# A four-part transformer block on one core: the second half of the tokens moved beside the first half's expert chunks

## The reference, cut to what matters

```python
x = x + tanh(g_xattn[0]) * wkv(w, u, k=layernorm(x), v=ctx)          # scan over the 256 tokens of a sequence
x = x + tanh(g_ffn[0])   * ffn(layernorm(x))                         # 256 -> 1024 -> 256, ternary weights, 8-bit activations
x = x + tanh(g_xattn[1]) * attention(layernorm(x), ctx)              # 32 heads of 8, rms-normed q and k, softmax over 256 keys
x = x + tanh(g_ffn[1])   * moe(layernorm(x))                         # 64 experts of width 64, top 8, one shared expert

def moe(x):
    logits = x @ gate_w.T
    W = softmax over the top 8 logits, zero elsewhere                # (tokens, 64)
    gate, up = x @ gu_w                                              # every expert on every token
    out = (silu(gate) * up * W) @ dp_w
    return out + sigmoid(x @ sh_gate1_w.T) * shared_expert(x)
```

## Time and profile before

| | us |
|---|---|
| runs before (3) | 525.39 median, 525.39 to 528.26 |
| the profiled execution | 525.49 |
| its span, from the first to the last record | 523.7 |
| busy PE / DVE / ACT / POOL | 405.8 / 340.7 / 293.1 / 23.7 |
| mean granted clock of PE | 0.94 |
| DMA | 38.01 MB, mean 73 GB/s |

### The profile page before, as it was taken

The page is one execution under the profiler, slowest core; times in us unless marked ns, Lnnn a source line. Parts: engine busy times, 40 slices in busy tenths (PEclk is TensorE's granted clock), DMA queues, the critical chain, the costliest instruction groups (busy, mean ns, idle before and its releaser), DMA issues.

```text
span 523.7 us, 7357 instructions
## 1 busy us (share of the span) xinstructions
PE 405.8 (77%) x2606; PEld 194.0 (37%) x2606; DVE 340.7 (65%) x723; ACT 293.1 (56%) x447; POOL 23.7 (5%) x21
## 2 busy tenths in 40 slices
PE   1104237448666798877799999999999999999994
PEld 1002123225443343433345444444444444444442
DVE  6899399884875554756497477566565565554553
ACT  2992894757787889887455254443333434423321
POOL 0002051002000111000000000000000000000000
PEclk9999856968999889998799999999999999999999
DMA  8400000000002000004520345633433433312211
GB/s 308 167 0 0 1 0 1 1 0 1 0 3 61 0 3 2 2 11 130 169 83 26 108 129 166 175 101 113 141 103 109 140 111 102 131 60 72 70 61 40
DMA packets 24576, 38.01 MB, mean 73 GB/s; under 512 B 4826, under 2 KB 11354, under 8 KB 24028
## 3 DMA queue, kind: packets, MB, share of 16 engines
q1 hardware_dynamic: 24540, 37.54, 22.7%
HBM read 36.21 MB, written 1.31 MB: 72 GB/s over the span
## 4 chain that ended last, share of the span: by engine, by line
PE 58%; ACT 16%; DVE 14%; issue 8%; DMA 2%; POOL 1%; SPq 1%; ACTq 0%; DVEq 0%
PE ps L1133 34%; PE ps L1406 15%; ACT regA L639 4%; ACT regA L467 1%; PE ps L1125 1%; PE ps L1190 1%; ACT regA L470 1%; PE ps L1155 1%; PE ps L1333 1%; DVE xn L762 1%; DMA regA<-in_dp_dram 1%; PE ps L1290 1%; DVE bn L748 1%; DMA x<-in_x_dram 1%; ACT regB L531 1%
## 5 line engine op out<-in xcount | busy, mean ns | idle before, releaser
L1133 PE MATMUL ps<-hH,regB 128*128 128x512 f16 x512 | 164.0, 382 | 0.0
L691 ACT ACTIVATE regA<-ps 128x512 f32<-128x512 f32 x65 | 38.8, 597 | 146.7 <-PE ps L1133 144.9
L1091 DVE TENSOR_TENSOR regA<-ps,regA 128x512 f32<-128x512 f32 x65 | 45.0, 692 | 100.2 <-ACT regA L691 100.2
L1133 PE MATMUL ps<-hL,regB 128*128 128x512 f16 x256 | 97.8, 382 | 0.0
L1406 PE MATMUL ps<-regA,regB 128*128 128x512 f16 x384 | 93.3, 379 | 1.3 <-DVE regA L1096 1.3
L1133 PEld LDWEIGHTS ps<-hH,regB 128*128 128x128 f16 x512 | 50.4, 98 | 61.7 <-issue 2.9
L639 ACT ACTIVATE regA<-ps 128x1024 f32<-128x1024 f32 x64 | 62.0, 1025 | 10.0 <-PE ps L1320 9.1
L1406 PEld LDWEIGHTS ps<-regA,regB 128*128 128x128 f16 x384 | 37.3, 98 | 47.3 <-DVE regA L1096 2.4
L1096 DVE TENSOR_TENSOR regA<-regA 128x512 f16<-128x512 f32 x65 | 44.3, 682 | 0.7 <-ACT regA L683 0.7
L1101 DVE TENSOR_TENSOR regA<-regA 128x512 f32<-128x512 f32 x65 | 44.5, 685 | 0.0
L683 ACT CAST regA<-regA 128x512 f16<-128x512 f32 x65 | 39.6, 610 | 1.5 <-DVE regA L1101 1.5
(11 more groups left out here) (169 smaller groups left out, 498.4 us busy)
## 6 DMA issues: line engine op xcount, KB each, us to landing
regA<-routing_dram SPq DMA_DIRECT2D x130, 128.0 KB, 3.1
regA<-in_gu_dram SPq DMA_DIRECT2D x32, 256.0 KB, 2.6
regA<-in_dp_dram SPq DMA_DIRECT2D x32, 128.0 KB, 2.7
regA<-in_ffn_dram SPq DMA_DIRECT2D x2, 1024.0 KB, 8.2
x<-in_x_dram SPq DMA_DIRECT2D x2, 512.0 KB, 3.9
ctxT<-in_ctxT_dram SPq DMA_DIRECT2D x1, 1024.0 KB, 8.2
regB<-in_ffn_dram SPq DMA_DIRECT2D x1, 1024.0 KB, 12.2
out_dram<-x SPq DMA_DIRECT2D x2, 512.0 KB, 3.3
```

The source lines that it names most:

```text
L691: nc.scalar.activation(sgm[:, c % 2, :], bank(GATE_BANK[c % 2]), ACT.Silu, scale=UNSCALE).then_inc(esilu_done, 1)
L1091: V.tensor_tensor(sgm[:, c % 2, :], bank(GATE_BANK[c % 2] + 1), sgm[:, c % 2, :], ALU.mult).then_inc(et_done, 1)
L1133: mm = T.matmul(out_ap, w(k), a(k), start=(n == 0), stop=(n == 3 * DK - 1))
```

## The change

It rewrites the order of the whole kernel. What is computed, and in what precision, stays the same but for two roots (below).

1. Halves. All stages up to the routing run for the first half of the tokens (tiles 0 to 3), with the second half's scan between its attention groups and the second half's wide products of tile 4. Then the chunks start: 32 pairs on half 0, the shared expert, 32 pairs on half 1. Beside chunks 0 to 27 lie the second half's FFN (tiles 5 to 7 and the rest of 4), its q and k/v projections, its 32 score units and 16 weighted values, heads, norms and routing. Three tables say what each engine does in places A, B and C of a chunk.
2. Weights. NW is 9. 8 pairs are kept from half 0 to half 1; the other 24 are fetched and split again (57 entries instead of 33).
3. Banks. In chunks 0 to 32 gate and up have banks 2 and 3 alone (every chunk), half 0's accumulators 0 and 1, the beside work 4 to 7. From chunk 33 on they alternate between 6, 7 and 2, 3; half 1's accumulators are 4 and 5. Gate and up now signal one by one.
4. Table loads. In chunks 11 to 22 and 26 silu is computed by tanh (same table as exp): ACT's tanh(z/2), DVE (1 + tanh) * gate, then times up: one more DVE operation.
5. POOL has no work. Row splits go to DVE (`split_low`); the ternary weights are clamped on DVE (`ternary_weights`, five operations of 2048 columns), with one ACT Relu; `drop_magic` goes. Second-half row turns are copied out by ACT. For scan chunks 2 and 3 DVE clamps (`clamps`) what ACT's Relus of the second pair did.
6. From norm 8 and row run 4 on, the inverse root starts from an integer guess on DVE (`bits_root`) and takes three Newton steps there, without ACT.

```diff
-        SHARED = NW
-        CHUNKS = [(p, 0) for p in range(NW)] + [(p, 1) for p in range(NW)] + [(SHARED, 2)]
-        CHUNKS += [(p, h) for p in range(NW + 1, PAIRS - NW) for h in range(2)]
-        CHUNKS += [(p, 0) for p in range(PAIRS - NW, PAIRS)] + [(p, 1) for p in range(PAIRS - NW, PAIRS)]
+        KEPT = NW - 1
+        LATER = [SHARED - KEPT + j for j in range(KEPT)] + list(range(SHARED - KEPT))
+        CHUNKS = [(p, 0) for p in range(SHARED)] + [(SHARED, 2)] + [(p, 1) for p in LATER]
...
+        ENTRY_PAIR = list(range(PAIRS)) + LATER[KEPT:]
+        SPLIT_AT = {e: e - EARLY if e < PAIRS else e + 4 for e in range(EARLY, ENTRIES)}
+        for e in range(NS + EARLY, ENTRIES):
+            LOAD_IN[SPLIT_AT[e - NS] + 3] = e
...
+        BESIDE_SCALAR = {
...
+            (10, "B"): [("table_exp_tanh",), ("probabilities", 32, 4), ("probabilities", 33, 6)],
+            (11, "A"): [("probabilities", 34, 4), ("probabilities", 35, 6)],
...
+        BESIDE_VECTOR = {
...
+            (5, "C"): [("row_sums", 10), ("row_sums", 11), ("rows", 5), ("norm", 9)],
...
+            (7, "C"): [("split_low", 11), ("row_sums", 12), ("row_sums", 13), ("weights_low", 10), ("rows", 6)],
...
+            (10, "C"): [("row_sums", 15), ("split_low", 13), ("rows", 7)],
...
+            (22, "C"): [("heads_sum", 31, 5), ("low_halves", 10, 6), ("weights_low", 28), ("heads_out", 6, 4),
+                ("heads_out", 7, 6), ("stats", 11), ("norm", 11)],
...
+        BESIDE_PRODUCTS = {
...
+            (5, "B"): [("project", 10, 7), ("project", 11, 6)],
+            (5, "C"): [("project", 12, 7), ("project", 13, 6)],
...
+            (13, "A"): [("scores", 39, 6), ("weighted_values", 18, 5)],
...
+        BY_TANH = tuple(range(11, 23)) + (26,)
+
+        def gate_bank(c):
+            return 6 if c > SHARED and (c - SHARED) % 2 else 2
+
+        ACC = (0, 4)
...
+            def bits_root(src, n, mul, eps, gain):
...
+                link(V.tensor_scalar(v, src, mul / gain ** 2, eps / gain ** 2, ALU.mult, ALU.add))
+                link(V.tensor_scalar(t.bitcast(I32), v.bitcast(I32), 1, None, ALU.logical_shift_right))
+                link(V.tensor_scalar(r.bitcast(I32), t.bitcast(I32), -1, ROOT_GUESS, ALU.mult, ALU.add))
+                for i in range(3):
+                    link(V.scalar_tensor_tensor(t, r, -0.5, v, ALU.mult, ALU.mult))
+                    link(V.tensor_tensor(t, t, r, ALU.mult))
+                    link(V.scalar_tensor_tensor(r, t, 1.5, r, ALU.add, ALU.mult))
...
+            def experts_product(c):
+                dve.wait_ge(esilu_done, c + 1)
+                rows = sgm[:, c % 2, :]
+                if c in BY_TANH:
+                    V.scalar_tensor_tensor(rows, rows, 1.0, bank(gate_bank(c)), ALU.add, ALU.mult).then_inc(ea_done, 1)
+                    dve.wait_ge(ea_done, 1 + BY_TANH.index(c))
+                dve.wait_ge(eup_done, c + 1)
+                V.tensor_tensor(rows, bank(gate_bank(c) + 1), rows, ALU.mult).then_inc(et_done, 1)
...
             for c in range(NCH + 1):
...
+                if c < NCH:
+                    experts_product(c)
+                beside(c, "A")
                 if c >= 1:
+                    experts_low(c - 1)
+                beside(c, "B")
                 if c < NCH:
+                    experts_weighted(c)
+                beside(c, "C")
...
+            def experts_in(c, i):
...
+                b = gate_bank(c) + i
+                take(b, (esilu_done, c + 1) if i == 0 and c not in BY_TANH else (et_done, c + 1))
...
             for c in range(NCH + 2):
                 if c < NCH:
+                    experts_in(c, 0)
+                beside(c, "A")
+                if c < NCH:
+                    experts_in(c, 1)
+                beside(c, "B")
                 if c >= 2:
                     experts_out(c - 2)
+                beside(c, "C")
```

More of the change, by code:

```diff
@@ L114, in bass_flamingo @@
[L114 to L123, removed]
@@ L321, in bass_flamingo, with row_tile, of_keys @@
[L321 to L327 removed]
+        BITS_RUN = 4
+        def row_tile(n):
+            return 2 * (n // 4) + n % 2
+        def of_keys(n):
+            return n % 4 < 2
+        NG = B * GROUPS
+        NGH = NG // 2
@@ new lines, in _ @@
+            heads_sum(9, 3)
+            heads_sum(10, 2)
+            stats(6)
+            weights_low(0)
+            weights_low(1)
+            norm(5)
+            heads_sum(11, 3)
+            norm(6)
+            heads_sum(12, 2)
+            token_scales(1)
+            heads_sum(13, 3)
+            rows(4)
+            heads_sum(14, 2)
+            heads_sum(15, 3)
+            low_halves(5, 6)
+            split_low(8)
+            heads_out(2, 2)
+            split_low(9)
+            heads_out(3, 6)
@@ new lines, in logits @@
+            def logits(h, b):
+                take(b, (LG_ready, h + 1))
+                pe.wait_ge(hL_ready, halves_before((7, 11)[h]) + DK)
+                for j in range(HT):
+                    t = h * HT + j
+                    n = 0
+                    for k in range(DK):
+                        for a in (hH, hL):
+                            for w in (gateH, gateL):
+                                mm = T.matmul(bank(b)[:, j * P:j * P + E + 1], a[:, k, t * P:(t + 1) * P], w[:, k, :],
+                                              start=(n == 0), stop=(n == 4 * DK - 1))
+                                n += 1
+                mm.then_inc(logit_done, 1)
@@ new lines, in turn_weights, with sum_weights @@
+            def turn_weights(h, b):
+                take(b, (WT_ready, h + 1))
+                pe.wait_ge(W_ready, h + 1)
+                for j in range(HT):
+                    mm = T.transpose(bank(b)[0:E + 1, j * P:(j + 1) * P], Wf[:, j, :], identf[:, :])
+                mm.then_inc(W_turned, 1)
+            def sum_weights():
+                pe.wait_ge(const_set, 1)
+                pe.wait_ge(abs_done, 3)
+                take(7, (ws_ready, 1))
+                T.matmul(bank(7)[:, 0:3], ones, asum[:, 0:3], start=True, stop=True).then_inc(abs_summed, 1)
@@ new lines, in _ @@
+            narrow(1, 6)
+            turn_hidden(2, 2)
+            turn_hidden(3, 4)
+            turn_norm(2, 6)
+            narrow(2, 1)
+            narrow(3, 3)
+            project(2, 5)
+            project(3, 7)
+            turn_rows(0, 6)
+            project(4, 5)
+            turn_rows(1, 7)
+            project(5, 4)
+            turn_norm(3, 5)
+            turn_rows(2, 7)
+            turn_rows(3, 6)
+            scores(0, 4)
+            scores(1, 6)
+            scores(2, 2)
```

1659 lines of the change are left out of this document (1010 added, 649 removed).

## The result

The changed kernel takes 495.04 us (median), the one before 526.83 in the same series: a ratio of 0.940, 95% interval 0.934 to 0.945. The forecast was 498 us in a range of 479 to 524. The profiled execution took 494.66 us for a span of 492.9. One of the four runs took 576.88 us at a mean granted clock of 0.743 instead of 0.943 to 0.946; the ratio leaves it out, and without it the median is 494.94 us.

A forecast was written before the change was run, and what follows sets the result against it. PE was taken to bound the stage behind chunk 0's start; ahead of it no engine was full. P 166 + 269.1 + B 46.7 + s 14 = 495.8 us of span, plus 1.8, gave 498 us, range 479 to 524.

The forecast's parts named there:

- P: The time at which expert chunk 0 starts: 254.6 us before the change, forecast 166 us.
- B: Second-half PE work that moves from ahead of chunk 0 to beside chunks 0 to 26: forecast 46.7 us.
- s: New PE idle time behind chunk 0's start: forecast 14 us, ends 3 and 27.
- all of before behind chunk 0: The old kernel's span from chunk 0's start to the end, carried over unchanged: 269.1 us.
- the share of 0.80: DVE's busy share from the first half's FFN end to chunk 0: 71 us of work would take 89 us.
- tight rival: The written order keeps all three engines full: DVE share 0.90, s = 5, total 477 us; chance 0.17.
- late start rival: First-half attention is a latency chain, DVE share stays 0.58: P = 197, total 529 us, no change; chance 0.17.
- the round trip of the routing weights: Store and broadcast load, 3.1 us each way, that DVE meets in chunk 0: 5 us of s.
- 9 us for lag: Chunks 0 to 32: DVE's excesses over PE sum to 18 us; with one chunk of lag allowed, half stays in s.
- What was costed at nothing: The 24 second weight splits in chunks 37 to 60, given no time; 7 us if PE waited for each.
- The stretch: Ahead of chunk 0, DVE operations slowed while GpSimd works: about 9 us of DVE time go with GpSimd's work.
- That nothing overlaps: Rival: a wait on the second half's products holds the chunks back; about 516 us; chance 0.02.

The follow-up runs named there:

- experiment 6: The changed kernel with ten more DVE multiplications spread over the first half's steps ahead of chunk 0: 504.53 us, 9.5 more.
- experiment 7: The changed kernel with the first four row-turn copies, ahead of chunk 0, on ACT instead of DVE: 496.11 us, 1.1 more, within the noise.
- experiment 11: The changed kernel with the lone score units of chunks 11 to 13 and 18 to 20 put in pairs on PE: 496.65 us, 1.6 more.
- experiment 3: The changed kernel with one more DVE multiplication in each of chunks 0 to 8 alone: 500.99 us, 6.0 more.
- experiment 4: The changed kernel with two Newton steps instead of three behind the integer guess, in eight roots on DVE: 491.80 us, 3.2 less.
- experiment 5: The changed kernel with DVE's beside group of place A ahead of the product of silu and up, no work added: 513.11 us, 18.1 more.
- experiment 8: The changed kernel without the second fetch and second split of 24 weight pairs: 495.18 us, 0.1 more.
- experiment 9: The changed kernel with the 16 row splits given back to GpSimd, the clamps left on DVE: 500.28 us, 5.2 more.
- experiment 10: The kernel before the change with GpSimd's row splits and clamps on DVE: 522.74 us against 526.79, ratio 0.994.
- experiment 12: The changed kernel with silu never computed by tanh, so ACT loads tables to and fro between silu and exp: 520.30 us, 25.3 more.
- experiment 2: The changed kernel with one more DVE multiplication in each of chunks 0 to 32: 504.25 us, 9.2 more.

## Why the prediction was right

Each term against its measure:

| term | forecast | measured |
|---|---|---|
| P, chunk 0's start | 166 | 162.3 (162.3 to 166.1 in seven profiles) |
| B, PE work moved behind it | 46.7 | 53.6 |
| s, new PE idle time | 14 | 7.9 |
| all of before behind chunk 0 | 269.1 | 269.1 (taken over) |
| span | 495.8 | 492.9 |

**P.** Its first part, the chain to the end of the first half's FFN, was put at 75 us; the last residual ends at 75.97. DVE's work ahead of chunk 0 was put at 136 us and is 139.1, but 60.4 of it lie in the first part (65 forecast) and 78.7 in the second (71 forecast). At the share of 0.80 that I took, 78.7 us would have lasted 98. The share was mis-sized: it is 0.91, that of the tight rival, and the second part lasts 86.3 us instead of 89 + 2. So P came out by two errors that cancel, some 8 us too little work in the second part and a share that is too low there, and not by a right working. Experiments 6 and 7 bear on it: added DVE work shows in full there, and the little that was taken off came back as waits for ACT. The late start rival is out: its 0.58 was the share of an attention stage with nothing beside it.

**B.** 6.9 us too small, most of it by the lone score unit. I had priced units that follow each other, 0.18 each; between other work one takes 0.32 us of its own and 0.10 more of the product ahead of it (start, duration):
```profile
232.80 0.38 PE L1562 MATMUL ps<-hH,regW 128*128 128x512 f16 x1
233.12 0.39 PE L1655 MATMUL ps<-regO,KT 32*128 32x256 f16 x4
233.44 1.25 PE L1892 MATMUL ps<-regW 128*128 128x512 f16 x5
```
In all L1655 is busy 10.7 us behind chunk 0 instead of 32 x 0.18 = 5.8, 4.9 more, and experiment 11 moved PE's busy time by 2.5 us with pairs alone. The page of the kernel before had warned of it: 19.9 us for its 64 units, 0.31 each, part of it at the lower clock:
```profile
L1320 PE MATMUL ps<-regA,KT 32*128 32x256 f16 x256 | 19.9, 280 | 9.9 <-ACT regA L639 7.6
```
The other pieces came out near their prices. Weighted values behind a chunk product lengthen that one by 0.10 us too, eight times; the rest of the miss, about 1 us, is spread over the products and was not followed.

The clock adds almost nothing to it. PE begins chunk 0 at the lower clock level, 1.2 GHz, after a stretch in which it was busy two thirds of the time at a granted clock of 0.83. Its products start 0.42 us apart until 166.6, then 0.22:
```profile
162.34 0.62 PE L1562 MATMUL ps<-hH,regW 128*128 128x512 f16 x1
162.75 0.63 PE L1562 MATMUL ps<-hL,regW 128*128 128x512 f16 x1
...
166.58 0.38 PE L1562 MATMUL ps<-hL,regW 128*128 128x512 f16 x1
```
But the kernel before begins its chunk 0 in the same way. The first 9.7 us behind chunk 0's start, first after, then before, with granted clocks of 0.78 and 0.81:
```profile
162.34:172.00 9.66, 9.66 (x53) 4.52 (x51) 8.62 (x35) 8.37 (x15) 0.00 (x0) 0.78 0.05 15
```
```profile
254.60:264.30 9.70, 9.70 (x48) 4.93 (x45) 4.77 (x9) 3.25 (x5) 0.00 (x0) 0.81 0.66 187
```
That costs 2.1 us after and 1.8 before. The prediction gave the lower level no time of its own, but 1.8 us of it were in the 269.1 that it took over; 0.3 us is new.

**s.** 6.1 us too large. Of its parts, 5 us for the round trip of the routing weights did not come: none of PE's waits names it, and none of DVE's up to 200 us. The 9 us for lag look like the measured 7.9, but by luck: they were argued as waits for DVE's product in two banks, and those are 0.7 us in the changed kernel. PE's waits are for norms and residuals of the beside work and for DVE's low part (4.8 us), and for ACT (3.0), which the sum had at nothing. DVE's load in the stage was forecast as 155 us and is 157. Experiments 3 and 4 show that DVE's lag costs PE time in the early chunks, whatever it waits for; experiment 5 shows the path that was argued: if the product comes a group later, the lag turns into PE's wait for it.

**What was costed at nothing** held: the 24 second splits (experiment 8). **GpSimd** held in sign; the exchange is worth 4 to 5 us from either side (experiments 9 and 10). The stretch, put at 9 us of DVE time, can be read from experiment 10: DVE took over 14 splits at 0.60 start to start and three clamps of 1.22, 12.1 us, and was busy only 2.8 us longer up to chunk 0 (182.87, not 180.04), so 9.3 us of stretch went. The clamping of the ternary weights, taken as 6 us, is 2 x 1.22 + 3 x 0.69 = 4.5.

**The tanh part** was weighed only as 13 operations more on DVE. That was its small side: what it saves, 24 table loads on ACT, is worth 25 us (experiment 12). The forecast did not fall by it, since it priced the kernel with tanh, but a reader of it would not have known which of the edits carries the result.

So the direction and the ledger held: the two owners, the overlap, the second splits at nothing. That the time came out only 3 us under the forecast is in part luck: errors of 7 us (B) and 6 us (s) stand against each other, and P's 3.7, itself no larger than the spread of the start, hides two of its own. Of the other rivals, the tight one had the right share for DVE; its 477 is 18 us too low, 8 by P (DVE had more work there), 7 by B and 3 by s. That nothing overlaps is ruled out by the chunk stage's rows. A slip without effect: 65 chunks of 3.88 us are 252.2 us, not 252.5.

## What to carry to other kernels

When latency-bound work is moved beside a compute-bound loop, price it twice: its engine time on the loop's bound engine, which stays (53.6 of 92.3 us here, with 7.9 of new idle time beside it), and its order, which only works with the loop around it. In the loop's own queue put first what frees the buffer that the bound engine needs next; small groups of work ahead of it cost 18 us here without a single added instruction. Price a small piece as it will stand, alone between others: a score unit cost 0.42 us so, 0.18 in a row of its like. Look for the fullest second engine stretch by stretch: the same added operation cost 0.85 of its time in the early chunks and 0.25 in the late ones. Taking work away paid likewise in the early chunks, but not in the start, where it made DVE wait for ACT. And count what a reordering does to table loads: here 24 of them were worth most of the gain.

## What the runs showed of the hardware

**Idle time of PE costs more than its length.** In experiment 5 the chunk stage grew by 15.0 us, but PE's idle time in it only by 11.4 (20.1 instead of 8.7): the other 3.6 us are the same work at a lower clock, 0.97 instead of 0.99 in the mean. In experiment 2 it was 5.2 of idle and 2.8 of clock. Experiment 5 has two waits of 4.57 and 4.06 us, which end at 177.63 and 188.78 us, and the granted clock is at the lower level around each end:
```profile
177.43:180.84 3.41, 3.21 (x10) 1.64 (x11) 0.83 (x2) 0.00 (x0) 0.00 (x0) 0.50 0.78 259
...
187.67:194.50 6.83, 5.72 (x21) 3.66 (x22) 1.58 (x5) 1.24 (x2) 0.00 (x0) 0.50 0.00 0
```
The Trainium skill (TensorE: Matmul & The Clock Gate, Part 1) has the array fall back to half clock when it has been idle; by that rule, the trace agrees.

**GpSimd can stretch one-input operations too.** In experiment 9, beside a pair of splits from 98.89 us on, a DVE operation with one tensor input took 1.37 us, where the next of its kind took 0.48:
```profile
100.25 1.37 DVE L1068 TENSOR_SCALAR regW<-regW,nwkv 128x512 f32<-128x512 f32 x1
...
103.88 0.48 DVE L1068 TENSOR_SCALAR regW<-regW,nwkv 128x512 f32<-128x512 f32 x1
```
I had counted only operations with two SBUF inputs. The Trainium skill (SBUF — State Buffer, the section on two separate sides) names a second kind, a DVE operation in a two-port mode; 0.48 us for 512 columns, against 0.69 with two inputs, would fit that, and no run here separates it further.

**A switch of tables costs the load alone.** ACT's timeline in experiment 12:
```profile
261.48 1.28 ACT L758 ACT_TABLE_LOAD   x1
262.77 0.60 ACT L948 ACTIVATE regW<-ps 128x512 f32<-128x512 f32 x1
263.39 1.28 ACT L755 ACT_TABLE_LOAD   x1
264.68 1.02 ACT L723 ACTIVATE regF<-ps 128x1024 f32<-128x1024 f32 x1
```
The next operation starts 0.01 us after the load's end, and the load 0.02 us after the operation ahead of it. The first holds for every load behind chunk 0, the second for all that did not wait for PE. The Trainium skill (ScalarE: Activation LUTs, What ACT_TABLE_LOAD costs) has 1283 ns for the load, as here, and another 1380 ns for a drain; of the drain the trace shows nothing, and the measurement decides: 1.3 us a switch in this kernel.
